# Twenty-nine products of a cleared tile on TensorE ahead of the first z, in a two-layer feed-forward and attention kernel

## What is computed

```python
x = x + 0.5 * ffn(layernorm(x))
x = x + attn(layernorm(x))
x = x + 0.5 * ffn(layernorm(x))

def ffn(x):                       # 8 experts of 256 x 256, top 2
    logits = x @ router_w + router_b
    vals, idx = top_k(logits, 2)
    full_w = sum(one_hot(idx, 8) * softmax(vals)[..., None], axis=-2)
    h = einsum('td,edf->etf', x, expert_w) + expert_b[:, None, :]
    combined = einsum('etf,te->tf', silu(h), full_w)
    y = x + combined @ proj_w + proj_b
    return norm_w * (y / sqrt(mean(y * y) + 1e-6))
```

## Time and profile before

| what | value |
|---|---|
| median of 3 runs | 827.48 us (825.24 to 830.95) |
| the profiled execution | 827.55 us |
| its span, first to last instruction | 825.8 us |
| mean granted TensorE clock over the span | 0.987 |
| TensorE busy with products | 792.3 us (96%) |
| VectorE, ScalarE, GpSimd busy | 651.9, 507.4, 517.2 us |

### The profile page before, as it was taken

The page is one execution under the profiler, slowest core; times in us unless marked ns, Lnnn a source line. Parts: engine busy times, 40 slices in busy tenths (PEclk is TensorE's granted clock), DMA queues, the critical chain, the costliest instruction groups (busy, mean ns, idle before and its releaser), DMA issues.

```text
span 825.8 us, 16045 instructions
## 1 busy us (share of the span) xinstructions
PE 792.3 (96%) x4712; PEld 697.7 (84%) x4712; DVE 651.9 (79%) x1917; ACT 507.4 (61%) x1250; POOL 517.2 (63%) x408
## 2 busy tenths in 40 slices
PE   7899999859999999999999999999999999999996
PEld 4688878658999999999899998999999988788885
DVE  6988996886677686786866868768687799988876
ACT  3565565567667586675765767557576586444543
POOL 4636648693878778787777777877878761112302
PEclk9999999978999999999999999999999999999998
DMA  9245412201132122212312313132131110000001
GB/s 295 86 135 191 148 58 52 52 13 39 27 77 73 41 51 76 51 25 64 102 26 50 88 30 85 27 88 51 31 96 25 39 27 1 1 1 26 2 26 52
DMA packets 28998, 50.09 MB, mean 61 GB/s; under 512 B 3874, under 2 KB 9634, under 8 KB 28962
## 3 DMA queue, kind: packets, MB, share of 16 engines
q1 hardware_dynamic: 28964, 49.67, 21.5%
HBM read 18.72 MB, written 9.96 MB: 35 GB/s over the span
## 4 chain that ended last, share of the span: by engine, by line
PE 82%; DVE 6%; POOL 5%; ACT 3%; issue 2%; DMA 1%; SPq 0%; POOLq 0%; DVEq 0%; ACTq 0%
PE pt L1696 8%; PE pj L1631 5%; PE pj L1633 5%; PE pj L1632 5%; PE o L1710 5%; PE o L1711 4%; PE o L1712 4%; PE sc L1685 4%; PE sc L1684 4%; PE sc L1683 4%; PE pj L1740 4%; PE pj L1742 3%; PE pj L1741 3%; PE sc L973 3%; PE sc L975 3%; PE sc L974 3%
## 5 line engine op out<-in xcount | busy, mean ns | idle before, releaser
L1260 POOL TENSOR_TENSOR at_ql<-at_rot,at_qh 128x512 fp32r<-128x512 f32 x64 | 82.7, 1292 | 103.0 <-ACT at_qh L1485 102.9
L1387 DVE TENSOR_TENSOR at_ptl<-pt,at_pth 128x512 fp32r<-128x512 f32 (+1 forms) x192 | 108.9, 595 | 45.9 <-ACT at_pth L1532 45.6
L1532 ACT ACTIVATE at_pth<-pt 128x512 fp32r<-128x512 f32 (+1 forms) x192 | 94.0, 525 | 81.9 <-PE pt L1696 81.9
L1526 ACT ACTIVATE at_pr<-at_pr,at_low 128x512 f32<-128x512 f32 (+3 forms) x256 | 140.5, 557 | 3.0 <-DVE at_low L1373 2.9
L1272 POOL TENSOR_TENSOR at_rot<-at_rot,gc 128x512 f32<-128x512 f32 x80 | 103.3, 1291 | 6.3
L1382 DVE TENSOR_SCALAR at_pr<-at_pr,at_inv 128x128 f32<-128x128 f32 (+3 forms) x256 | 105.3, 473 | 2.3
L1268 POOL TENSOR_TENSOR at_rot<-ga,cos 128x512 f32<-128x512 f32 x80 | 104.5, 1307 | 2.3 <-POOL at_ql L1260 2.3
L1270 POOL TENSOR_TENSOR gc<-gc,sin 128x512 f32<-128x512 f32 x80 | 103.9, 1299 | 1.0 <-DMA gc<-ga 1.0
L1373 DVE CUSTOM_DVE_ANT_0 at_pr<-sc,at_mask 128x512 f32<-128x512 f32 (+2 forms) x192 | 100.8, 549 | 0.4 <-PE sc L1685 0.3
L1696 PE MATMUL pt<-ident,at_pr 128*128 128x128 f32 x640 | 93.6, 277 | 6.8 <-DVE at_ptl L1387 5.1
L1485 ACT ACTIVATE at_qh<-at_rot 128x512 fp32r<-128x512 f32 x64 | 40.6, 634 | 95.9 <-POOL at_rot L1272 95.9
(11 more groups left out here) (282 smaller groups left out, 2263.6 us busy)
## 6 DMA issues: line engine op xcount, KB each, us to landing
gc<-ga SPq DMA_DIRECT2D x160, 128.0 KB, 2.3
ga<-in_attn_w SPq DMA_DIRECT2D x8, 384.0 KB, 4.8
gb<-attn_split SPq DMA_DIRECT2D x6, 512.0 KB, 4.2
at_wo<-attn_split SPq DMA_DIRECT2D x6, 512.0 KB, 4.3
attn_split<-gb SPq DMA_DIRECT2D x6, 384.0 KB, 2.4
attn_split<-gc SPq DMA_DIRECT2D x6, 384.0 KB, 3.3
x<-in_x SPq DMA_DIRECT2D x4, 512.0 KB, 9.3
e_raw<-in_expert_w SPq DMA_DIRECT2D x8, 256.0 KB, 6.2
```

What stands on the lines that cost most here:

```text
L1387: dve.tensor_tensor(ptl[h % 2][:, cols], pt[(NF * h + k) % 2][:, 0:FLEN[k]], pth[h % 2][:, cols].bitcast(F32), ALU.subtract).then_inc(lo_d ...
L1526: act.activation(pr[h % 2][:, cols], pr[h % 2][:, cols], ACT.Exp, bias=low[h % 2][:, i:i + 1], scale=-1.0, accum_out=tot[h % 2][:, i:i + 1 ...
```

## The change

A helper `warm_up(count)` is added to TensorE's program. It multiplies a part of the cleared tile `r_hl` (128 x 128 as the stationary factor) with the whole of it (256 columns as the moving factor) into the bank `sc0`, `count` times, and adds 1 to a new semaphore `warmed` at the end. It is called with 7 once the tile is cleared (`setup` at 1), ahead of the wait for `e_row`, and with 22 after the first two row products, ahead of the transposes. VectorE waits for `warmed` to reach 2 before it writes the router weights into `r_hl`.

```diff
@@ -148,7 +148,7 @@
-            tables_in, step_done = sem("tables_in"), sem("step_done")
+            tables_in, step_done, warmed = sem("tables_in"), sem("step_done"), sem("warmed")
@@ -646,6 +646,7 @@
                 shift_pair(0)
                 dve.wait_ge(cols_in, 16)
                 dve.wait_ge(setup, 2)
+                dve.wait_ge(warmed, 2)
                 dve.tensor_copy(r_hl[:, :, 0:E], r_raw).then_inc(r_split, 1)
                 dve.tensor_copy(r_h0[:, :, 0:E], r_raw).then_inc(r_split, 1)
                 dve.wait_ge(r_split, 2)
@@ -901,6 +902,12 @@
+            def warm_up(count):
+
+                for n in range(count):
+                    r = pe.matmul(ex_ps[1][:, 0:C * P], r_hl[:, 0, :], r_hl[:].rearrange("p c k -> p (c k)"), start=True, stop=True)
+                r.then_inc(warmed, 1)
+
             def row_of(p):
@@ -1064,9 +1071,12 @@
             if first:
+                pe.wait_ge(setup, 1)
+                warm_up(7)
                 pe.wait_ge(e_row_in, 16)
                 row_of(0)
                 row_of(1)
+                warm_up(22)
                 pe.wait_ge(ident_in, 16)
                 transpose_first_z()
                 row_of(2)
```

## The result

The changed kernel takes 829.37 us as the median of 22 runs (827.79 to 833.3), the kernel before 826.21 in 22 runs beside it (825.06 to 830.98). The ratio is 1.0031 with a 95% interval of 1.0019 to 1.0044: slower by 0.3%, some 2.6 us (the two medians differ by 3.2; the ratio is the one on record, not their quotient). Forecast were 828.5 in a range of 825.0 to 831.5, against 827.5, that is plus 1.0.

A forecast was written before the change was run, and what follows sets the result against it. TensorE, busy for most of the 825.8 us span, was taken as the bound; fillers outlasting the wait for z move GpSimd's second shift by +1.24, less 0.26 for the tanh: 827.55 + 1.0 = 828.5 us, range 825.0 to 831.5.

The forecast's parts named there:

- The rise at 10.4: TensorE's clock rises 3.4 us after 7.0, within the 22 fillers, which end at 11.1; chance 0.50.
- The seven: First fillers, before the row products: 1.5 us from about 1.65 to 3.2; row products start 0.55 us later, needed by nobody.
- The router (4 x 0.23), row_of(3) (about 1.0) and logits_back end by 17: TensorE work behind the transposes runs at the high clock; nothing waits for it, VectorE comes to the logits at 18.67.
- the tanh: ScalarE is free earlier for it, so VectorE's 0.26 us wait at 22.07 goes: 1.24 - 0.26 = +1.0 us.
- GpSimd holds VectorE: `gap` on VectorE takes 1.24 us because GpSimd's shift of expert weights holds the shared port pair; both end at 19.7.
- The prediction's other sum: If `gap`'s 1.24 us were its own, it would end at 20.77 instead of 20.93, making the sum 0.9 us.
- The wait on VectorE at no cost: VectorE's wait for `warmed` holds the router-weight casts until 11.1, but z_rest behind them waits for ScalarE until 12.9 anyway.
- A fall in the new gap at 19.6: TensorE waits from near 19.6 to 22.9 before the second expert pair; the clock may fall; priced 0, upper end 0.5.
- All of it between 150 and 200: Mean granted clock 0.987 means 21 us at the low level, all claimed to lie in that stretch.
- the clock rises only with the real products: Rival: fillers of zeros or into an unread bank do not count; the 22 end at 11.7, time 830.8 us; chance 0.13.
- The clock's later falls: Rival: one low-clock stretch more or fewer between 150 and 200 us decides, 830.2 or 826.8 us; chance 0.20.
- The early rise: Rival: clock rises before or at the 22, which end at 9.6; the change pays, 827.0 us; chance 0.17.

The follow-up runs named there:

- the second profile: The changed kernel run and profiled again without any edit; 828.31 us in this one run.
- own tile, ones: Against the change: fillers read a separate tile, set to ones by GpSimd, with no VectorE wait for warmed; 829.17 us against 826.30 before, ratio 1.0019.
- 12 ahead of the router: Against the change: fillers read a separate zeroed tile without the VectorE wait, plus 12 products behind row_of(2); 828.20 us against 826.30 before, ratio 1.0017.

## Why the prediction was right or wrong

Right were the sign, the range and the mechanism: the fillers are longer than their wait, the transposes start late, and the delay goes to the end. "Within 1%" holds. The range says little, since no change at all (826.2) would have been in it too. That 828.5 lies only 0.9 us from 829.37 is luck: the median of before is 826.21 in 22 runs, 1.3 below the 827.48 of the three that I started from.

The size was too small, 1.0 for 2.6 by the ratio and 2.7 at the landmark. By one of its own signs the prediction was wrong: the transposes start at 11.97, in the second profile at 12.01, after the 11.8 that it had set as the latest. The sum with the measured terms is 3.53 (11.97 against 8.44) less 0.8 given back at the transposes, 2.7 at the copy and 2.7 at the landmark. The steps that failed are these.

- *The rise at 10.4.* It came at 11.9, in the last of the 22, and in the second profile behind them. The transposes started at 11.97 for 11.1, ScalarE's copy at 12.93 for 12.03: 0.9 of the missing 1.7. I had the value from one rise in the earlier trace rows, took its 3.5 us as typical, and called it "low before". It was not: the column falls at 155.9, 0.1 us after products began there. The profiles with a long row of fillers show 4 to 6 us from the first of the row. The bound without a rise, 11.7, was 0.3 short: the 22 began at 7.15 for 7.0 and took 4.82 for 22 x 0.213 = 4.69, nearly all at the low step.
- *The seven.* 1.5 us were worked out, 1.79 were taken (1.65 to 3.44), 0.3 more than seven steps. The row products ended 0.2 later and the 22 began at 7.15 instead of 7.0.
- *"The router (4 x 0.23), row_of(3) (about 1.0) and logits_back end by 17."* The clock fell at 15.3, in the stretch between the transposes and the router where TensorE has only a row product and 1.2 us idle. I looked for a fall only at the experts' second pair. So the logits came at 20.2, VectorE still waited 0.90, row_of(3) still bound GpSimd's second shift, which began at 19.97 for 18.55, and the tanh gave nothing. This is the other 0.8 of the sum; but in the two profiles in which the clock held until 24 (own tile, ones; 12 ahead of the router) only 0.2 of it was won, since my step from GpSimd's shift to the landmark left out that the shift then holds VectorE at an earlier operation.
- *GpSimd holds VectorE.* `gap` took 1.24 us again and ended with GpSimd's shift at 22.35; the run with fillers ahead of the router shows it from the other side. The rule of the Trainium skill on the shared port pair ("SBUF — State Buffer", section "SBUF: two separate sides") agrees with the row of `gap`, which has two SBUF inputs. The operation that took 2.37 has one, and the rule holds such an operation only in a 2-port mode; no row here shows the mode. The prediction's other sum, for a 1.24 us that were `gap`'s own, comes to 0.8 and not to 0.9 (20.77 - 19.72 - 0.26).
- *The wait on VectorE at no cost.* The casts did wait, 1.92 us, and z_rest behind them waited for ScalarE anyway (0.87 more). It holds.
- *A fall in the new gap at 19.6.* There was no such gap in the change, since the router was late. With the clock held it appears, 3.2 to 3.6 us before the second pair. The clock fell in it in the kernel whose fillers end before z (20.5), and 0.6 and 1.0 us behind its end in the other two (24.1 and 24.8).
- *"All of it between 150 and 200."* Of the low time of the first profile 17.1 us lie there; the rest is at the end, from 821.5 on.

Of the rivals, "the clock rises only with the real products" (plus 3.3 us) is the one whose steps the change followed most closely, since the 22 ran at the low step but for the last, though not its cause: the fillers did raise the clock, late enough to serve the transposes and no dense product. "The clock's later falls" has a fitting number too (830.2, plus 2.7), but the profile of the change has less low time between 150 and 200 us than that of before, not more. How much the later falls add to the medians of the change was not measured. "The early rise" needs fillers that end before z; placed so, they cost nothing and bring nothing that 10 runs can show.

## What to carry to other kernels

Filler in a wait must end when the wait does: read its length and multiply out the step at the low clock, not at the high one, since here the clock rose 4 to 6 us behind the first of a long row of fillers, and not at the same place in two profiles of one kernel. Before adding any, follow what comes behind the wait: here the next dense products were 3.3 us away, the clock was down again by then, and VectorE and GpSimd, not TensorE, set the pace. Compare a single profile with a second one of the same kernel before reading a microsecond out of it.

## What the runs showed of the hardware

- Row products of two partitions kept TensorE busy for 4.3 us, behind 3.7 us of the same, and the clock did not rise until 24.1, with the experts. In the kernels with 22 or more fillers in a row it rose between 6.9 and 13.05; with fillers of ones at 10.5, of zeros in the same tile at 10.8.
- The transposes do run at the high level where it is granted: step 0.11 for 0.21.
- The clock fell at 15.3 although TensorE had never been idle for more than 1.2 us since 1.65.
- The column of the granted clock says 1.00 from the start of every profile here, though products step at 0.43 until the first rise. What the engine does is read from the step there.
- A VectorE operation of 0.17 us took 2.37 beside GpSimd's.
